# A node-wise dense stage of a graph network: six buffers for x, and products of the older block ahead of transposes of the newer

## What is computed

```python
deg = segment_sum(ones, row);  dis = deg ** (-0.5)
norm = dis[row] * dis[col]
agg = segment_sum(h[col] * norm[:, None], row)
out = relu(agg @ W.T + b)
return h + out          # the caller adds x: x + (h + out)
```

## Time and profile before

| | us |
|---|---|
| three runs | 7485.44, 7486.71, 7510.91 |
| median | 7486.71 |
| span of the profiled execution | 7497.3 |
| the stage in it, first load issued to last R | 1678.0 to 2236.5 |

### The profile page before, as it was taken

The page is one execution under the profiler, slowest core; times in us unless marked ns, Lnnn a source line. Parts: engine busy times, 40 slices in busy tenths (PEclk is TensorE's granted clock), DMA queues, the critical chain, the costliest instruction groups (busy, mean ns, idle before and its releaser), DMA issues. The chain is left out here.

```text
span 7497.3 us, 113351 instructions
## 1 busy us (share of the span) xinstructions
PE 3517.3 (47%) x18429; PEld 2636.7 (35%) x18429; DVE 5174.6 (69%) x20258; ACT 2902.8 (39%) x7124; POOL 5022.1 (67%) x4720
## 2 busy tenths in 40 slices
PE   7655256646658888850005777200786233333000
PEld 1111155546656666640004555100564122222000
DVE  7999488877778888877776777322674355555554
ACT  0366111117764333335555666100232255554222
POOL 0377578874447777776657774577787677776577
PEclk9756599998889999985557888655998555555555
DMA  7488577769983333346669999322897333333343
GB/s 288 161 289 288 150 137 142 141 124 277 286 251 92 92 91 92 90 109 175 176 169 349 361 363 330 97 52 50 301 343 241 94 102 103 103 103 95 120 136 114
DMA packets 1168522, 1326.52 MB, mean 177 GB/s; under 512 B 231275, under 2 KB 968789, under 8 KB 1157938
## 3 DMA queue, kind: packets, MB, share of 16 engines
q1 hardware_dynamic: 961680, 1002.76, 41.8%
q0 software_dynamic: 206768, 323.00, 17.8%
HBM read 706.30 MB, written 646.54 MB: 180 GB/s over the span
## 5 line engine op out<-in xcount | busy, mean ns | idle before, releaser
L690 POOL DMA_INDIRECT dense<-t_xs,ends x784 | 789.0, 1006 | 360.3 <-issue 182.2
L1810 PE MATMUL ps<-dense,w 128*128 128x256 f32 x3136 | 731.1, 386 | 187.2 <-DVE dense L1519 160.2
L530 POOL DMA_INDIRECT t_src<-tot,sidx x392 | 626.8, 1599 | 183.4 <-issue 94.6
L1810 PEld LDWEIGHTS ps<-dense,w 128*128 128x128 f32 x3136 | 581.4, 190 | 305.2 <-DVE dense L1519 193.8
L1732 PE MATMUL ps<-oneh_c,oneh_p 128*128 128x395 f16 x1568 | 458.7, 430 | 276.2 <-DVE oneh_c L867 267.1
L762 ACT ACTIVATE estd<-emv,epsc 128x2 f32<-128x2 f32 (+1 forms) x588 | 174.1, 296 | 1044.2 <-DVE emv L745 1044.2
L1519 DVE SCALAR_TENSOR_TENSOR dense<-xT 128x256 f32<-128x256 f32 x1568 | 544.6, 419 | 3.6 <-ACT xT L1991 3.4
L665 POOL DMA_INDIRECT t_yacc<-dense,gq x392 | 456.1, 1164 | 129.6 <-issue 111.1
L690 POOL DMA_INDIRECT dense<-t_y,ends x392 | 372.9, 951 | 251.2 <-DVE ends L1612 164.7
L628 POOL DMA_INDIRECT out_rows<-dense,sidx x392 | 387.9, 990 | 183.1 <-issue 111.6
L628 POOL DMA_INDIRECT t_xs<-dense,sidx x392 | 398.5, 1017 | 123.7 <-issue 65.2
(11 more groups left out here) (327 smaller groups left out, 12111.5 us busy)
## 6 DMA issues: line engine op xcount, KB each, us to landing
dense<-t_xs SPq DMA_DIRECT2D x78, 1320.0 KB
dense<-in_x SPq DMA_DIRECT2D x156, 640.0 KB
t_xs<-dense SPq DMA_DIRECT2D x98, 528.0 KB, 4.5
t_xs<-hb SPq DMA_DIRECT2D x78, 660.0 KB, 6.1
t_src<-dense SPq DMA_DIRECT2D x99, 512.0 KB, 6.3
t_sum<-dense SPq DMA_DIRECT2D x98, 512.0 KB
t_src<-dense SPq DMA_DIRECT2D x78, 640.0 KB, 3.3
dense<-t_src SPq DMA_DIRECT2D x78, 640.0 KB
```

The lines of the kernel that those rows point to most:

```text
L530: gp.indirect_dma_start(t_src, bass.IndirectOffsetOnAxis(ap=sidx[:, p.k, c:c + 1], axis=0), tot[:, p.k, c, :], None, compute_op=ALU.add).t ...
L690: gp.indirect_dma_start(rows[:, p.k, c, :], None, table, bass.IndirectOffsetOnAxis(ap=gidx[:, p.k, c:c + 1], axis=0)) \
L1810: i = nc.tensor.matmul(ps[:, o:o + 2 * P], w1[:, k, :], xm[:, p.w, k, :], start=(k == 0), stop=(k == R - 1))
```

## The change

- x gets six places: the three of before and areas 9 to 11 of `dense`. x(n) now waits for X(n-6).
- A new `wide_loop` runs turns of six blocks and writes out the first 18. All five streams of the stage use it.
- SP's order in a step is the store with lag 4, then the sums, then x. Before it was x, sums, and then the store with lag 3.
- TensorE's order in a step is the products with lag 1, then the transposes with lag 0. Before it was the other way round.
- VectorE waits for the old store of its `hb` slot between Z and R, and no longer ahead of Z. Its lag in the loop falls from 1 to 0, which moves nothing, as it has one stage only.
- ScalarE's function is split in two, called in the same order. GpSimd still adds x to h.

```diff
-            def conv0_load(r, u, p):
-                if needed(b - SLOTS + 1):
-                    sp.wait_ge(L0["xh"].sem, L0["xh"].after(b - SLOTS + 1))
-                sp.dma_start(xin[u][0:p], rows_of(x, b, p)).then_inc(L0["ld"][u].sem, 16)
...
-            node_loop(sp, (conv0_load, 0), (conv0_store, 3))
+            def conv0_x(w, p):
+                if needed(w.b - WIDE + 1):
+                    sp.wait_ge(L0["gain"].sem, L0["gain"].after(w.b - WIDE + 1))
+                sp.dma_start(xin0[w.u][0:p], rows_of(x, w.b, p)).then_inc(X0["load"][w.u].sem, 16)
...
+            wide_loop(sp, (conv0_store, 4), (conv0_sums, 0), (conv0_x, 0))
...
-                if needed(r):
-                    v.wait_ge(L0["sto"][u].sem, L0["sto"][u].after(r * 16))
                 v.wait_ge(L0["mm"].sem, L0["mm"].after(b + 1))
...
                 i.then_inc(L0["z"].sem, 1)
+                if needed(w.n):
+                    v.wait_ge(L0["sto"][u].sem, L0["sto"][u].after(w.n * 16))
                 v.wait_ge(L0["z"].sem, L0["z"].after(b + 1))
...
-            node_loop(pe, (conv0_turn, 0), (conv0_mm, 1))
+            wide_loop(pe, (conv0_mm, 1), (conv0_turn, 0))
...
-            node_loop(a, (conv0_first, 0))
+            wide_loop(a, (conv0_first, 0), (conv0_h, 0))
```

More of the change, by code:

```diff
@@ L131, in node_loop_back, with __init__, wide_loop, at @@
                 fn(r - back if back else r, u - lag + back * SLOTS, P)
+    for b in range(NB, NB + 1 + most):
+        at(b)
+WIDE = 2 * SLOTS
+assert NB % WIDE == 0
+class Wide:
+    def __init__(self, r, u):
+        while u < 0:
+            r, u = r - 1, u + WIDE
+        self.r, self.u = r, u
+        self.b = r * WIDE + u
+        self.k, self.n = u % SLOTS, r * 2 + u // SLOTS
+def wide_loop(eng, *stages):
+    most = max(lag for _, lag in stages)
+    peeled = (2 * WIDE + most + WIDE - 1) // WIDE
+    def at(b):
+        for fn, lag in stages:
+            if 0 <= b - lag <= NB:
+                fn(Wide((b - lag) // WIDE, (b - lag) % WIDE), PT if b - lag == NB else P)
+    for b in range(peeled * WIDE):
+        at(b)
+    with eng.Fori(peeled, NB // WIDE) as r:
+        for u in range(WIDE):
+            for fn, lag in stages:
+                fn(Wide(r, u - lag), P)
     for b in range(NB, NB + 1 + most):
@@ L319, in gnn @@
         xin = [area(i) for i in range(3)]
+        xin0 = xin + [area(9 + i) for i in range(3)]
         ain = [area(3 + i) for i in range(3)]
@@ L463, in gnn @@
         R0 = phase("runs", NPAIR, "", SC)
-        L0 = phase("node", NB + 1, "nm h tr trc mm z xh res",
-                   {"ld": slots(16), "lda": slots(16), "sto": slots(16)})
+        L0 = phase("node", NB + 1, "nm h tr trc mm z gain res", {"lda": slots(16), "sto": slots(16)})
+        X0 = phase("rows", NB + 1, "", {"load": [16 * len(range(u, NB + 1, WIDE)) for u in range(WIDE)]})
         E1 = phase("edge", NPAIR, "ring bn mv std rs nb h tx txc masked xw relu back", GP)
@@ L967, in _, with conv0_sums, conv0_store @@
             end_phase(sp, SP)
-            def conv0_load(r, u, p):
-                b = r * SLOTS + u
-                if needed(b - SLOTS + 1):
-                    sp.wait_ge(L0["xh"].sem, L0["xh"].after(b - SLOTS + 1))
-                sp.dma_start(xin[u][0:p], rows_of(x, b, p)).then_inc(L0["ld"][u].sem, 16)
[L974 to L983, removed]
-            node_loop(sp, (conv0_load, 0), (conv0_store, 3))
+            def conv0_x(w, p):
+                if needed(w.b - WIDE + 1):
+                    sp.wait_ge(L0["gain"].sem, L0["gain"].after(w.b - WIDE + 1))
+                sp.dma_start(xin0[w.u][0:p], rows_of(x, w.b, p)).then_inc(X0["load"][w.u].sem, 16)
+            def conv0_sums(w, p):
+                if needed(w.b - SLOTS + 1):
+                    sp.wait_ge(L0["tr"].sem, L0["tr"].after(w.b - SLOTS + 1))
+                sp.dma_start(ain[w.k][0:p], rows_of(t_src, w.b, p)).then_inc(L0["lda"][w.k].sem, 16)
+            def conv0_store(w, p):
+                sp.wait_ge(L0["nm"].sem, L0["nm"].after(w.b + 1))
+                sp.wait_ge(L0["res"].sem, L0["res"].after(w.b + 1))
+                sp.dma_start(t_xs[bass.ds(w.b * BR, p * K), XW1:2 * XW1].rearrange("(p k) f -> p k f", k=K), hb[w.k][0:p]) \
+                    .then_inc(L0["sto"][w.k].sem, 16)
+            wide_loop(sp, (conv0_store, 4), (conv0_sums, 0), (conv0_x, 0))
             stored(sp, L0, 16)
@@ L1149, in _, with conv0_xh @@
             end_phase(gp, PO)
[L1151 to L1155, removed]
+            def conv0_xh(w, p):
+                gp.wait_ge(L0["h"].sem, L0["h"].after(w.b + 1))
+                gp.tensor_tensor(ob_h[w.k][0:p], xin0[w.u][0:p], ob_h[w.k][0:p], ALU.add).then_inc(L0["gain"].sem, 1)
+            wide_loop(gp, (conv0_xh, 0))
             end_phase(gp, PO)
@@ L1467, in _, with conv0_rest @@
             end_phase(v, VE)
-            def conv0_rest(r, u, p):
-                b = r * SLOTS + u
-                if needed(r):
-                    v.wait_ge(L0["sto"][u].sem, L0["sto"][u].after(r * 16))
+            def conv0_rest(w, p):
+                b, u = w.b, w.k
                 v.wait_ge(L0["mm"].sem, L0["mm"].after(b + 1))
@@ L1478, in conv0_rest @@
                 i.then_inc(L0["z"].sem, 1)
+                if needed(w.n):
+                    v.wait_ge(L0["sto"][u].sem, L0["sto"][u].after(w.n * 16))
                 v.wait_ge(L0["z"].sem, L0["z"].after(b + 1))
-                v.wait_ge(L0["xh"].sem, L0["xh"].after(b + 1))
+                v.wait_ge(L0["gain"].sem, L0["gain"].after(b + 1))
                 nc.vector.scalar_tensor_tensor(out=hb[u][0:p, :, 0:D], in0=oa[u][0:p], scalar=0.0, in1=ob_h[u][0:p],
@@ L1493, in _ @@
                                            op0=ALU.mult, op1=ALU.add, accum_out=carried[:, 1:2])
-            node_loop(v, (conv0_rest, 1))
+            wide_loop(v, (conv0_rest, 0))
             end_phase(v, VE)
@@ L1765, in _, with conv0_turn, conv0_mm @@
             end_phase(pe, PE)
[L1767 to L1771, removed]
+            def conv0_turn(w, p):
+                pe.wait_ge(L0["lda"][w.k].sem, L0["lda"][w.k].after(w.n * 16 + 16))
+                if needed(w.b):
+                    pe.wait_ge(L0["trc"].sem, L0["trc"].after(w.b))
                 for k in range(K):
-                    i = nc.tensor.transpose(ps[:, k * P:k * P + p], ain[u][0:p, k, :], ident[0:p, 0:p])
+                    i = nc.tensor.transpose(ps[:, k * P:k * P + p], ain[w.k][0:p, k, :], ident[0:p, 0:p])
                 i.then_inc(L0["tr"].sem, 1)
[L1776 to L1780, removed]
+            def conv0_mm(w, p):
+                pe.wait_ge(L0["trc"].sem, L0["trc"].after(w.b + 1))
+                if needed(w.b):
+                    pe.wait_ge(L0["z"].sem, L0["z"].after(w.b))
                 for k in range(K):
-                    i = nc.tensor.matmul(ps[0:p, ZC + k * P:ZC + (k + 1) * P], fT[u][:, k, 0:p], w0t[:, :],
+                    i = nc.tensor.matmul(ps[0:p, ZC + k * P:ZC + (k + 1) * P], fT[w.k][:, k, 0:p], w0t[:, :],
                                          start=True, stop=True)
@@ L1959, in turned, with conv0_first, conv0_h @@
                                      func, bias=bias).then_inc(signal.sem, 1)
[L1961 to L1964, removed]
+            def conv0_first(w, p):
+                turned(L0["trc"], w.b, p, fT[w.k], K, L0["tr"], L0["mm"])
+            def conv0_h(w, p):
+                b, u = w.b, w.k
+                a.wait_ge(X0["load"][w.u].sem, X0["load"][w.u].after(w.r * 16 + 16))
                 if needed(b - SLOTS + 1):
@@ L1967, in conv0_first @@
                 for k in range(K):
-                    i = nc.scalar.activation(ob_h[u][0:p, k, :], xin[u][0:p, k, :], ACT.Relu,
+                    i = nc.scalar.activation(ob_h[u][0:p, k, :], xin0[w.u][0:p, k, :], ACT.Relu,
                                              bias=mean_r[0:p, bass.ds(b * K + k, 1)],
@@ L1971, in conv0_first @@
                 i.then_inc(L0["h"].sem, 1)
-                if needed(r):
-                    a.wait_ge(L0["sto"][u].sem, L0["sto"][u].after(r * 16))
+                if needed(w.n):
+                    a.wait_ge(L0["sto"][u].sem, L0["sto"][u].after(w.n * 16))
                 nc.scalar.activation(hb[u][0:p, :, D], dis[1][0:p, bass.ds(b * K, K)], ACT.Copy).then_inc(L0["nm"].sem, 1)
```

## The result

| | before | after |
|---|---|---|
| median of four runs, us | 7498.8 (7485.4 to 7511.5) | 7417.8 (7406.1 to 7428.4) |
| span of the profiled execution, us | 7497.3 | 7413.1 |
| R to R in the stage, us a block | 6.90 | 5.78 |

The changed kernel is faster by 81 us, ratio 0.988 (95% interval 0.987 to 0.990; the two medians alone give 0.989). The forecast was 7457 in a range of 7436 to 7500, so the result lies outside and the gain is 2.7 times the 30 us forecast. In the profiled executions the whole gain is in the stage: (6.90 - 5.78) x 76 = 85 us of 84.

What follows compares the result with a forecast made beforehand. The prediction took a latency loop over three blocks, closely above a DMA limit, as the bound. Limits of 6.34 and 6.4 us plus 0.1 gave 6.5 us a block; (6.90 - 6.50) x 76 = 30 us, so 7457, range 7436 to 7500.

Steps and rivals of the forecast that it cites:

- The loop of three blocks before: Stage before: R to store, sums, T, M, Z, R; 20.65 us for three blocks, the whole pace of 6.90 us.
- T's wait: Sign on TensorE: T's wait for the sums from DRAM falls from 146 us per 500 to under 60.
- M was to wait: Sign on TensorE: M waits 80 to 130 us per 500 for C, where it waited 1.4 us.
- A sum: SP's loads: with sums ahead of x, they land about 7.2 us after R's end instead of 9.3.
- The DMA floor: Stage's transfers: 143.37 MB at 312 GB/s, so at least 6.34 us a block, a gain of 43 us at most.
- The prediction's own sign for this: Stage's DMA rate: the forecast is wrong on the floor if GB/s passes 325.
- Rival 2: Stage's transfers: the DMA floor isn't one; down to 5.9 us a block, 7411 us, halfway 7430; chance 0.10.
- The loop M, T, C, M: TensorE and ScalarE: single-block loop made by the new order, 6.4 us, bounds 5.4 and 8.2 by clock.
- ScalarE's C, H and copy: ScalarE's own loop: C 1.24, H 3.94, copy 0.2 and handovers, 5.6 us, under 6.34.
- Worth nothing by itself: Six places for x: the removed wait, 5.7 us in 3 waits, lay beside SP's wait for R; no gain.
- VectorE's loop, 5.9 us: VectorE: Z 2.7, R 3.0 including waiting for GpSimd's add, and 0.2; under 6.34.
- The sum: Stage: limits of 6.34 and 6.4 us alternate, 0.1 added, so 6.5 us a block, a gain of 30 us.

Runs made afterwards that it cites:

- e1: The kernel before with only TensorE's order changed (products of the older block, then transposes): 7441.1 us, ratio 0.992, 6.19 us a block.
- e2: The changed kernel with TensorE's order put back (transposes of the newer block first): 7467.2 us, ratio 0.996, 6.50 us a block.
- e7: The kernel before with half of x loaded in every block: 6.16 us a block.
- e9: The changed kernel without half of H's and half of M's instructions from the seventh block on, all transfers whole: 5.59 us a block at 355 GB/s.
- e8: The changed kernel with six extra unread products between T and M to hold the clock up: 7408.6 us, ratio 0.988, 5.68 us a block.
- e12: The changed kernel with the PSUM area handed between M and Z in three pieces, by bank: 7389.8 us, ratio 0.986, 5.62 us a block.
- e3: The changed kernel with x issued ahead of the sums again: 7405.4 us in one run, 5.78 us a block.
- e4: The changed kernel with three places for x instead of six: 7414.6 us in one run, 5.84 us a block.
- e10: The changed kernel with six places for sums, three for x, store lag 5, x lag 1, T ahead of M: 7427.7 us, ratio 0.990, 6.10 us a block.

## Why the prediction was wrong

- **The loop of three blocks before: right.** e1, e2 and e7 all act on it as it says. T's wait was to fall under 60 us per 500; it fell to 2.0 per 420. M was to wait 80 to 130 us per 500 for C; its weight loads wait 123.9 per 420, which is 147 per 500, and its products only 12.3. A sum is off by a little: with 0.44 and 2.1 us less, the sums land 6.8 us after R and not 7.2, which moves nothing.
- **The DMA floor: the step that failed.** The prediction divided the bytes by 312 GB/s, the rate of stretches in which "the engines never rest", and got 6.34 us and 43 us at most. In e9 the same packets go at 355, 5.59 us. The step read a busy share of 1.03 to 1.07 as full use. The prediction's own sign for this was a rate above 325; it is 339. Rival 2 had this outcome, with a chance of 0.10, 7430 halfway and 7411 at its far end; the measured 7418 lies between, while the pace of 5.78 lies past the 5.9 of that end.
- **The loop M, T, C, M: the second term, 6.4 us, mis-sized, and not the one that binds.** I kept the old mix, 3.13 and 1.57 us for M and T, on the ground that the gaps hardly shrink. Measured: M 204.1 us over 1443 instructions, 2.83, and T 96.6 over 730, 1.32; 2.83 + 1.32 + 1.24 + 0.45 is 5.8 where I had 6.4. Three handovers of 0.15 are too much as well, since T follows M with hardly a gap: at the high clock the loop took 4.8 us from M's start to C's end, where I had 5.4 in all. TensorE has one gap a block now, ahead of M (1.8 us in the mean, 2.2 at most); before nearly every T had one ahead of it (2.0 in the mean, up to 4.7). The clock went up to 0.92, not down. The prediction read from the earlier trace rows that gaps of one or two microseconds are enough to lose the clock sometimes. The length of the gap alone doesn't tell: with a gap of 1.88 us ahead of it M took 2.47 us at 2098.16 and 4.10 at 1975.10. With a gap left in every block the changed kernel's clock is 0.92 to 0.93, and with the gap filled (e8) it is 1.00. The waits for DMA fell as well, from 145.8 us per 500 to 2.0 per 420, and which of the two kinds of gap moved the clock from 0.84 to 0.93 isn't separated.
- **A loop that the prediction doesn't list.** M and Z take turns on the single PSUM area, 5.4 us at the high clock and 7.1 at the low. It sits in the rows of before too (M released by Z 21.1 us), small because the loop of three blocks hid it. It is the bound now, as e12 shows. M, T, C lies behind it at the high clock: from M's start at 2098.16, T ends at 2101.72 and C at 2103.00, 4.8 us. ScalarE's C, H and copy take 5.2 us (2096.32 to 2101.51), not 5.6.
- **"Worth nothing by itself": half right.** Six places and the swap each do nothing on top of the other (e3, e4). But the wait of 5.7 us in the earlier trace rows was that short only because SP stood at the store. With TensorE's new order the wait for x's place becomes 3.6 us a block (e1), 0.4 us of the pace. I priced a wait at what it cost under the old bound.
- **VectorE's loop, 5.9 us:** too long. I took R's mean of 3.0; where it doesn't meet GpSimd's add it is 1.49, as in every block of the changed kernel.
- **The sum** took two limits, 6.34 and 6.4. The first was too high by at least 0.75 us, the second by at least 0.6. Either one alone would have held the forecast near 6.4. That they agreed made them look safe.

## What to carry to other kernels

When a loop over buffers is opened, price every wait, clock mix and rate again under the new bound: those of the old trace are themselves results of the old bound. A transfer limit should be taken from a run in which the issuing engine hardly waits for the others, since a busy share at or above 1 doesn't show that the engines move all they can (1.03 at 307 GB/s before, 1.09 at 355 in e9). After opening a loop over blocks, look for the single buffers that two engines hand to each other; handing them over in pieces costs no memory, and here it took the block from 5.78 to 5.62 us.

## What the runs showed of the hardware

- A busy DMA share above 1.2 can mean little movement: 188 GB/s at 1.28 in the kernel before, against 355 GB/s at 1.09 in e9.
- R took 1.49 us in every block of the changed kernel, and 2.9 us in the middle case (up to 4.2) before, with the same operands. In every order with T ahead of M (before, e2, e7, e10) its mean in the window 1750 to 2100 us is 2.7 to 3.1 us. The difference goes with GpSimd's add. Of the 78 R over full blocks before, 71 began while an add ran, and each ended 1.34 to 1.44 us after that add; in the changed kernel none meets an add. One case: the add ran from 1961.32 to 1964.22 (row below), and R(38), begun at 1962.34, ended at 1965.57, 1.35 us after it. In 5 of the 78 the add began during R: R took 1.49 us and the add 4.05 to 4.24, where it otherwise takes 2.9.

```profile
1961.32 2.90 POOL L1154 TENSOR_TENSOR dense<-dense 128x1280 f32<-128x1280 f32 x1 [6.62 <-ACT dense L1968]
```

- SP's issue instruction for the sums has no fixed length: in the mean of the window 1750 to 2100 us it takes 1.1 us before (287 GB/s), 1.8 in the changed kernel (342), 3.2 in e12 (353) and 3.7 in e9 (355), but 0.4 in e1 (321). What lengthens it isn't separated. The profile lists waits for semaphores apart from it. One row of e12, against 1.16 us in the earlier trace rows:

```profile
1904.75 3.48 SPq L1011 DMA_DIRECT2D dense<-t_src  x1
```
